# A softmax whose exponentials move from one instruction per step to one per row

## The chip, the cores and the metric

The kernel runs on one core of one Trainium2 chip. The metric is the device time of one execution in microseconds (us).

## What is computed

A gated cross-attention layer and a gated expert layer over x (32 sequences x 64 positions x 512), all in fp32 precision:

```python
x = x + tanh(g_xattn) * attention(layernorm(x), ctx, ctx, mask)
x = x + tanh(g_ffn) * lora_top1(layernorm(x))
# attention: 32 query heads and 8 key/value heads of width 128, rotary embedding on q and k
raw    = einsum('bhqd,bhkd->bhqk', q, k) / sqrt(128)
attn   = softmax(raw + mask, axis=-1)        # over 64 keys
out    = einsum('bhqk,bhkd->bhqd', attn, v) @ wo
```

The softmax of one row of 64 scores is: find the maximum, subtract it, take exponentials, add them up, divide by the sum.

## The kernel before

The program is written with one instruction list per engine and semaphores between them. Engines are TensorE (PE, with its weight loads PEld), VectorE (DVE), ScalarE (ACT), GpSimd (POOL) and the DMA queue of SyncE (SP). Each list is executed in the order in which it is written. So an instruction that waits holds up all that stands behind it in its list.

Matmuls in fp32 precision are made of three products of a "high" half, which ACT writes as a rounded copy, and a "low" half, which DVE or POOL writes as the rest (`*_high`, `*_low`).

**First part (to about 238 us).** `JOBS`, 64 of them: keys and values of all sequences are made and stored in DRAM, and x is normalised, combined and turned. Beside them stand splits of the weights.

**Second part: 64 steps k** (`STEPS`). A step is one group of 4 heads, 4 sequences of 64 positions. Its scores fill one tile `prob` of 128 x 512: 128 partitions (two heads x 64 queries) and `ROWS` = 8 rows of 64 keys each. There is one such tile, and its steps reuse it. The steps are pipelined by one. In step k the lists hold, in this order:

- PE: `scores(k)` (L784), `times_values(k-1)` (L811, L815), one or two blocks of `product` (L767: the queries of the next group of heads), `project_out(k-1, 0)` (L829), in even steps another `product`, `turn_probs(k)` (L795: transposes `prob`, and waits for `normalised`), `project_out(k-1, 1)`, the last `product`.
- DVE: `mask_scores(k)` (L1030 scale and mask, L1033 the negated maximum of each row), `attn_low(k-1)` twice (L1053, which `project_out` waits for), `sum_rows(k)` (L1037 the sums, L1039 their reciprocals), `q_sum` (L1011), `add_out` (L1065, waits for `project_out`), `q_rope` (L969, L974), `prob_low` twice (L1046), `add_out`, `q_rope`.
- ACT: `attn_high(k-1)` twice (L1290), in even steps `copy_product` (L1266), `exponential(k)` (L1274), `wq_split` (L1237) in even steps, `q_shift` (L1244, L1245), in even steps `copy_product`, `prob_high(k)` (L1281, L1282: four instructions), `q_shift`, and further copies and splits.
- POOL: `subtract_max(k)` (L1437), in the even steps to 24 `combine_weights` (L1396 to L1401), `normalise(k)` (L1442), in the first 26 steps `weight_low` (L1406), `by_sin` (L1431, which `q_rope` waits for).

The softmax of step k thus goes over three engines: DVE finds the maxima, POOL adds the negated maxima to the tile, ACT takes all 512 exponentials of a partition in one instruction, DVE adds up the rows and inverts the sums, POOL multiplies. From step 26 on no weights are left to be split. Steps 30 to 33 and 62 and 63 also hold parts of the expert layer, and steps 60 to 63 have no `product`.

Of the kernel before, what the change touches and what calls it, by code (L numbers as in the profile page):

```python
# [10 lines left out]
ACT = mybir.ActivationFunctionType  # L11
AX = mybir.AxisListType

P = 128
BATCH, SEQ, DM = 32, 64, 512
# [24 lines left out]
ROWS = HEAD_PAIRS * SUB_SEQS  # L40
# [115 lines left out]
def sums_of(k):  # L156

    early, middle, late = products_of(k)
    done = [i for b, i in early]
    after = [i for b, i in late]  # L160
    b = (early or [(0, 0)])[0][0]
    return ([(b, j) for j, s in enumerate(SUMS) if s[1] in done], [(b, j) for j, s in enumerate(SUMS) if s[1] in after])


def ropes_of(k):

    early, late = sums_of(k)
    pending = sums_of(k - 1)[1] if k else [(1, 3)]
    pending = [q for q in pending if q[1] == 3]
    rest = [q for q in late if q[1] != 3]  # L170
    if len(early) == 2:
        return early[:1], early[1:], rest
    return pending, early, rest
# [6 lines left out]
SCORES_AFTER = 62  # L180
# [67 lines left out]
def wo_late(k):  # L248

    G, r = divmod(k, 4)  # L250
    lot = [[GROUP * G + 2, GROUP * G + 3] if G else [], [GROUP * G + 4], [GROUP * G + 5], []][r]
    return [n for n in lot if n < HEADS] if G < KV_HEADS else []


def build(nc, x, ctx_T, mask, g_attn, g_ffn, wq, wk, wv, wo, routed_w, lora_b, table, out):
# [10 lines left out]
    with ExitStack() as stack:  # L266
# [3 lines left out]
        def sem(name):  # L270
            return stack.enter_context(nc.semaphore(name))

        def sb_at(offset, name, shape, dt=F32):
            return nc.alloc_sbuf_tensor_at(name, shape, dt, offset=offset)
# [30 lines left out]
        prob = sb_at(base + 141312, "prob", [P, 512])  # L305
# [3 lines left out]
        def sb(name, shape, dt=F32):  # L309
            offset = cursor[0]  # L310
            cursor[0] += (4 * int(np.prod(shape[1:])) + 31) // 32 * 32
            return sb_at(offset, name, shape, dt)
# [15 lines left out]
        neg_max = sb("neg_max", [P, 2, ROWS])  # L328
        row_sum = sb("row_sum", [P, 2, ROWS])
# [34 lines left out]
        shifted, exponentials, probs_high, v_high = sem("shifted"), sem("exponentials"), sem("probs_high"), sem("v_high")  # L364
# [3 lines left out]
        raw_low_v, x_low, q_summed = sem("raw_low_v"), sem("x_low"), sem("q_summed")  # L368
        ln_stats, ln_moments, ln_var, ln_done = sem("ln_stats"), sem("ln_moments"), sem("ln_var"), sem("ln_done")
        times_cos, rope_added, masked, max_found = sem("times_cos"), sem("rope_added"), sem("masked"), sem("max_found")  # L370
        summed, inverted, probs_low, v_low = sem("summed"), sem("inverted"), sem("probs_low"), sem("v_low")
        out_low, x1_added = sem("out_low"), sem("x1_added")
        top_found, top_ranked, rank_found, weight_set = sem("top_found"), sem("top_ranked"), sem("rank_found"), sem("weight_set")
        weighted, out_ready = sem("weighted"), sem("out_ready")

        power_set, ln_rstd, times_sin, less_max = sem("power_set"), sem("ln_rstd"), sem("times_sin"), sem("less_max")
        normalised, raw_low_g, wq_low = sem("normalised"), sem("raw_low_g"), sem("wq_low")
        wq_combined, x_combined = sem("wq_combined"), sem("x_combined")

# [548 lines left out]
        def _(e):  # L928
# [90 lines left out]
            by_row = prob[:, :].rearrange("p (r k) -> p r k", r=ROWS)  # L1019

            def mask_scores(k):
                u, s = divmod(k, SUBS)
                G, c, index = chunk_of(u)
                m = mask_sb[:, c, s * SUB_SEQS:(s + 1) * SUB_SEQS, :].rearrange("p b k -> p (b k)").unsqueeze(1).to_broadcast(
                    [P, HEAD_PAIRS, SUB_SEQS * SEQ])
                e.wait_ge(scored, k + 1)
                e.wait_ge(mask_in[c], 16 * (index // CHUNKS + 1))
                if k:
                    e.wait_ge(probs_turned, k)
                e.scalar_tensor_tensor(out=by_head, in0=score[:, :].rearrange("p (h n) -> p h n", h=HEAD_PAIRS),  # L1030
                                       scalar=SCALE, in1=m, op0=ALU.mult, op1=ALU.add).then_inc(masked, 1)
                e.wait_ge(masked, k + 1)
                e.tensor_reduce(neg_max[:, k % 2, :], by_row, AX.X, ALU.max, negate=True).then_inc(max_found, 1)  # L1033

            def sum_rows(k):
                e.wait_ge(exponentials, k + 1)
                e.tensor_reduce(row_sum[:, k % 2, :], by_row, AX.X, ALU.add).then_inc(summed, 1)  # L1037
                e.wait_ge(summed, k + 1)
                e.reciprocal(row_inv[:, k % 2, :], row_sum[:, k % 2, :]).then_inc(inverted, 1)  # L1039

            def prob_low(k):
# [71 lines left out]
            for n in range(len(JOBS)):  # L1113
# [17 lines left out]
                    x_lows(X_BESIDE[n - X_TURN])  # L1131
                if n == SCORES_AFTER:
                    mask_scores(0)
            sum_rows(0)
            for k in range(STEPS):
                early, late = sums_of(k)
                ropes = ropes_of(k)
                if k:
                    mask_scores(k)
                    attn_low(k - 1, 0)  # L1140
                    attn_low(k - 1, 1)
                    for n in wo_late(k - 1):
                        raw_low(("wo", n))
                    expert_norms_end(norms_of(k - 1))
                between(k, 0)
                between(k, 1)
                if k:
                    sum_rows(k)
                for q in early:
                    q_sum(*q)  # L1150
                between(k, 2)
                if k:
                    add_out(k - 1, 0)
                between(k, 3)
                for q in ropes[0]:
                    q_rope(*q)
                between(k, 4)
                prob_low(k)
                between(k, 5)
                if k:  # L1160
                    add_out(k - 1, 1)
                between(k, 6)
                for q in ropes[1]:
                    q_rope(*q)
                for q in late:
                    if q[1] != 3:
                        q_sum(*q)
                between(k, 7)
                for q in ropes[2]:
                    q_rope(*q)  # L1170
                for q in late:
                    if q[1] == 3:
                        q_sum(*q)
                between(k, 8)
                expert_norms_begin(norms_of(k))
            k = STEPS
# [18 lines left out]
        def _(e):  # L1195
# [74 lines left out]
                shift(ROPE_NO["q", b, j], q_tile(b, j))  # L1270

            def exponential(k):
                e.wait_ge(less_max, k + 1)
                e.activation(prob[:, :], prob[:, :], ACT.Exp).then_inc(exponentials, 1)  # L1274

            def prob_high(k):
                e.wait_ge(probs_turned, k + 1)
# [45 lines left out]
            for k in range(STEPS):  # L1323
                first, middle, last = products_of(k)
# [45 lines left out]
        def _(e):  # L1370
# [61 lines left out]

            by_row = prob[:, :].rearrange("p (r k) -> p r k", r=ROWS)

            def subtract_max(k):
                e.wait_ge(max_found, k + 1)
                e.tensor_tensor(by_row, by_row, neg_max[:, k % 2, :].unsqueeze(2).to_broadcast([P, ROWS, SEQ]),  # L1437
                                ALU.add).then_inc(less_max, 1)

            def normalise(k):  # L1440
                e.wait_ge(inverted, k + 1)
                e.tensor_tensor(by_row, by_row, row_inv[:, k % 2, :].unsqueeze(2).to_broadcast([P, ROWS, SEQ]),  # L1442
# [5 lines left out]
            for n in range(len(JOBS)):  # L1448
                for w in SPLITS_BESIDE.get(n, ()):
                    raw_low(w)  # L1450
                if n in X_BESIDE:
                    x_norms(X_BESIDE[n])
                if n in COMBINED_BESIDE:
                    combine_weights(COMBINED_BESIDE[n])
                for w in WQ_BESIDE.get(n, ()):
                    weight_low(*w)
                if JOBS[n][0] == "k":
                    by_sin(ROPE_NO[JOBS[n]])
                if n in ROPE_BESIDE:
                    by_sin(ROPE_NO["q", *ROPE_BESIDE[n]])  # L1460
                if n in X_BESIDE:
                    combine_x(X_BESIDE[n])
                if n == SCORES_AFTER:
                    subtract_max(0)
            normalise(0)
            for k in range(STEPS):
                ropes = ropes_of(k)
                pieces = weights_of(k)
                if k:
                    subtract_max(k)  # L1470
                if pieces and k % 2 == 0:
                    combine_weights(pieces[0][0])
                if pieces and k % 4 == 3:
                    weight_low(*pieces[0])
                if k:
                    normalise(k)
                if pieces and k % 4 != 3:
                    weight_low(*pieces[0])
                for q in ropes[0]:
                    by_sin(ROPE_NO["q", *q])  # L1480
                if pieces:
                    weight_low(*pieces[1])
                for q in ropes[1] + ropes[2]:
                    by_sin(ROPE_NO["q", *q])
                for n in wo_late(k):
                    raw_low(("wo", n))
                for t in norms_of(k):
                    inverse_std(("expert", t))
# [45 lines left out]
```

## Time and profile before

| | |
|---|---|
| median of 3 runs | 1208.34 us (1205.32 to 1209.72) |
| profiled execution | 1204.42 us, span 1202.4 us |
| mean granted TensorE clock | 0.981 |
| busy | PE 94%, PEld 77%, DVE 76%, ACT 53%, POOL 47% of the span |

The span is what the profile covers. The busy share of an engine is its busy time over the span. "Idle before" is the time that an engine stood still ahead of an instruction, and the arrow names what ended it. In the timeline each row is one instruction, or several of a kind in a row (x2, x4): start in us from the span's start, duration, engine and line, and what is written and read with the shape.

### The profile page before, as it was taken

What the parts mean: (1) busy time and instruction counts of PE and PEld (TensorE: products, weight loads), DVE (VectorE), ACT (ScalarE), POOL (GpSimd) and SP (SyncE); (2) the same over time, 40 slices, a digit from 0 to 9 for tenths busy, and PEclk for the clock granted to TensorE, in tenths of its full rate; (3) what the DMA queues carried; (4) which work ended last, traced back from release to release, by engine and by line L of the source; (5) the groups of instructions that cost most, each with busy time, mean ns of one, the idle gap of its engine ahead of it and who ended that gap; (6) DMA issues with size and microseconds to landing.
All of it is one profiled execution on the core that took longest, in us unless ns stands there. A gap on an engine that the chain in (4) does not pass through costs nothing.

```text
span 1202.4 us, 17218 instructions
## 1 busy us (share of the span) xinstructions
PE 1134.0 (94%) x5792; PEld 929.5 (77%) x5792; DVE 916.3 (76%) x1408; ACT 632.8 (53%) x1090; POOL 567.8 (47%) x517
## 2 busy tenths in 40 slices
PE   7899899879999999999999999999999999999786
PEld 6688787767777777777878777888888888887664
DVE  6773756768777777777888898887878888888574
ACT  6452345555666666666665544555555555545331
POOL 4650468766767676766654332333333333333210
PEclk9899999889999999999999999999999999999897
DMA  6859954384444454535359435453433424241101
GB/s 220 249 196 369 316 182 179 123 323 144 176 168 175 153 182 135 184 132 185 114 219 355 161 123 160 145 195 107 158 106 140 165 90 158 88 158 34 47 27 44
DMA packets 88902, 197.89 MB, mean 165 GB/s; under 512 B 8304, under 2 KB 41200, under 8 KB 82928
## 3 DMA queue, kind: packets, MB, share of 16 engines
q1 hardware_dynamic: 88816, 196.79, 47.7%
q8 instruction: 48, 0.79, 0.3%
q14 instruction: 38, 0.31, 0.1%
HBM read 113.92 MB, written 82.84 MB: 164 GB/s over the span
## 4 chain that ended last, share of the span: by engine, by line
PE 52%; DVE 15%; POOL 14%; issue 11%; ACT 4%; DMA 1%; SPq 1%; DVEq 0%; POOLq 0%; ACTq 0%
PE attn L829 19%; PE proj L767 13%; POOL rot L1431 4%; PE score L784 4%; PE attn L719 4%; DVE o_s L1053 2%; PE score L719 2%; DVE q_r L969 2%; POOL wq_s L1406 2%; PE turned L719 2%; DVE p_low L1046 2%; DVE acc L1065 2%; PE turned L795 2%; DVE prob L1030 1%; ACT p_high L1282 1%
## 5 line engine op out<-in xcount | busy, mean ns | idle before, releaser
L829 PE MATMUL attn<-wo_s,o_s 128*128 128x512 f32 x1536 | 388.8, 402 | 17.1 <-DVE o_s L1053 17.1
L829 PEld LDWEIGHTS attn<-wo_s,o_s 128*128 128x128 f32 x1536 | 283.3, 190 | 89.3 <-DVE o_s L1053 32.7
L767 PE MATMUL proj<-xB,wq_s 128*128 128x512 f32 x1344 | 344.9, 400 | 6.8 <-DVE q_r L1011 3.5
L1431 POOL TENSOR_TENSOR rot<-rot,tab 128x512 f32<-128x512 f32 x160 | 215.0, 1345 | 224.2 <-ACT rot L1245 224.1
L767 PEld LDWEIGHTS proj<-xB,wq_s 128*128 128x128 f32 x1344 | 249.3, 189 | 67.9 <-DVE q_r L1011 4.4
L974 DVE TENSOR_TENSOR q_r<-q_r,rot 128x512 f32<-128x512 f32 x128 | 125.1, 978 | 52.6 <-POOL rot L1431 41.6
L1437 POOL TENSOR_TENSOR prob<-prob,neg_max 128x512 f32<-128x512 f32 x64 | 66.9, 1045 | 179.9 <-DVE neg_max L1033 179.9
L1290 ACT ACTIVATE o_s<-attn 128x512 fp32r<-128x512 f32 x128 | 69.6, 596 | 149.1 <-PE attn L815 149.0
L1065 DVE SCALAR_TENSOR_TENSOR acc<-attn,gates_t,acc 128x512 f32<-128x512 f32 x128 | 96.1, 751 | 67.3 <-PE attn L829 65.3
L969 DVE TENSOR_TENSOR q_r<-q_r,tab 128x512 f32<-128x512 f32 x128 | 136.0, 1063 | 3.1 <-ACT rot L1245 3.0
L784 PEld LDWEIGHTS score<-k_r,q_r 128*128 128x128 f32 x1024 | 124.1, 191 | 7.0 <-issue 2.4
L784 PE MATMUL score<-k_r,q_r 128*128 128x64 f32 x1024 | 121.1, 271 | 0.0
L1244 ACT ACTIVATE rot<-q_r 64x512 f32<-64x512 f32 x128 | 80.8, 631 | 62.5 <-DVE q_r L1011 55.5
L1046 DVE TENSOR_TENSOR p_low<-turned,p_high 64x512 fp32r<-64x512 f32 x128 | 87.8, 686 | 30.7 <-ACT p_high L1282 29.1
L1442 POOL TENSOR_TENSOR prob<-prob,row_inv 128x512 f32<-128x512 f32 x64 | 66.9, 1046 | 85.5 <-DVE row_inv L1039 85.5
L1266 ACT ACTIVATE copies<-proj 128x512 f32<-128x512 f32 x96 | 57.5, 599 | 91.2 <-PE proj L767 91.0
L1281 ACT ACTIVATE p_high<-turned 64x512 fp32r<-64x512 f32 x128 | 76.0, 593 | 33.5 <-PE turned L795 29.6
L1011 DVE TENSOR_TENSOR q_r<-copies,proj 128x512 f32<-128x512 f32 x128 | 84.2, 678 | 0.8 <-PE proj L767 0.6
L1274 ACT ACTIVATE prob<-prob 128x512 f32<-128x512 f32 x64 | 40.4, 632 | 83.4 <-POOL prob L1437 83.4
L1053 DVE TENSOR_TENSOR o_s<-attn,o_s 128x512 fp32r<-128x512 f32 x128 | 81.9, 681 | 0.2 <-ACT o_s L1290 0.2
L1245 ACT ACTIVATE rot<-q_r 64x512 f32<-64x512 f32 x128 | 80.7, 631 | 1.5
L1282 ACT ACTIVATE p_high<-turned 64x512 fp32r<-64x512 f32 x128 | 76.0, 594 | 1.5
(118 smaller groups left out, 1398.9 us busy)
## 6 DMA issues: line engine op xcount, KB each, us to landing
wq_kept<-wq_s SPq DMA_DIRECT2D x16, 1792.0 KB, 6.5
wq_s<-wq_kept SPq DMA_DIRECT2D x16, 1792.0 KB, 8.3
v_kept<-vst SPq DMA_DIRECT2D x64, 256.0 KB, 4.1
v_s<-v_kept SPq DMA_DIRECT2D x128, 128.0 KB, 4.9
wo_kept<-wo_s SPq DMA_DIRECT2D x32, 512.0 KB, 2.9
wo_s<-wo_kept SPq DMA_DIRECT2D x32, 512.0 KB, 5.3
k_kept<-kst SPq DMA_DIRECT2D x32, 256.0 KB, 2.1
wq_raw<-in_wq SPq DMA_DIRECT2D x16, 512.0 KB, 7.8
```

The costliest lines, as they stand in the source:

```text
L719: last = e.matmul(b[:, :], stationary, moving, start=(kt == 0 and m == 0), stop=(kt == KT - 1 and m == 2))
L767: last = e.matmul(dst[:, :], wq_s[:, b % 2, A, s, kt, :], xB[:, B, mv, kt, :], start=(first and kt == 0 and m == 0), stop=(kt == 1 and m = ...
L784: last = e.matmul(score[:, col:col + SEQ], two_heads, k_r[:, u % 2, seq * SEQ:(seq + 1) * SEQ], start=True, stop=True)
L829: last = e.matmul(attn[bp][:, :], o_s[:, s, bp, h, :], wo_s[n % WO_SLOTS][:, m, :], start=(h == 0 and i == 0), stop=(h == GROUP - 1 and i ...
L969: e.tensor_tensor(dst, src, cos, ALU.mult).then_inc(times_cos, 1)
L974: e.tensor_tensor(dst, dst, by_seq(rotated(r)), ALU.add).then_inc(rope_added, 1)
L1011: e.tensor_tensor(q_tile(b, j), by_seq(copies[:, copy, :]), by_seq(proj[PRODUCTS[i][2]][:, :]), ALU.add).then_inc(q_summed, 1)
L1046: e.tensor_tensor(p_low[rows, :], turned[rows, :], p_high[rows, twin, :].bitcast(F32), ALU.subtract).then_inc(probs_low, 1)
L1053: e.tensor_tensor(low, src, high.bitcast(F32), ALU.subtract).then_inc(out_low, 1)
L1065: e.scalar_tensor_tensor(out=acc[:, tile, :], in0=attn[bp][:, :], scalar=gates_t[:, 0:1], in1=acc[:, tile, :], op0=ALU.mult, op1=ALU.add). ...
L1282: e.activation(p_high[rows, twin, :], turned[rows, :], ACT.Copy).then_inc(probs_high, 1)
L1431: e.tensor_tensor(r3, r3, sin, ALU.mult).then_inc(times_sin, 1)
```

## The change

The three passes over the tile (subtraction on POOL, one exponential on ACT, sums on DVE) are replaced by eight ACT instructions, one for each row of 64. Each takes the row's negated maximum as a per-partition bias and writes the row's sum as a second result. The reciprocals (L1039) and the multiplication (L1442) stay. The semaphores `less_max` and `summed` go.

```diff
             def exponential(k):
-                e.wait_ge(less_max, k + 1)
-                e.activation(prob[:, :], prob[:, :], ACT.Exp).then_inc(exponentials, 1)
+                e.wait_ge(max_found, k + 1)
+                for r in range(ROWS):
+                    here = prob[:, r * SEQ:(r + 1) * SEQ]
+                    last = e.activation(here, here, ACT.Exp, bias=neg_max[:, k % 2, r:r + 1],
+                                        accum_out=row_sum[:, k % 2, r:r + 1])
+                last.then_inc(exponentials, 1)
...
-            def sum_rows(k):
+            def invert_sums(k):
                 e.wait_ge(exponentials, k + 1)
-                e.tensor_reduce(row_sum[:, k % 2, :], by_row, AX.X, ALU.add).then_inc(summed, 1)
-                e.wait_ge(summed, k + 1)
                 e.reciprocal(row_inv[:, k % 2, :], row_sum[:, k % 2, :]).then_inc(inverted, 1)
...
-            def subtract_max(k):
-                e.wait_ge(max_found, k + 1)
-                e.tensor_tensor(by_row, by_row, neg_max[:, k % 2, :].unsqueeze(2).to_broadcast([P, ROWS, SEQ]),
-                                ALU.add).then_inc(less_max, 1)
...
-                if n == SCORES_AFTER:
-                    subtract_max(0)
...
-                if k:
-                    subtract_max(k)
```

The call `sum_rows(k)` becomes `invert_sums(k)` at the same place of DVE's list, and `exponential(k)` keeps its place in ACT's.

## Rows read from the trace of the kernel before

**Rows 1.** The page's busy times: us, share of span, instructions.

```profile
PE 1134.0 (94%) x5792; PEld 929.5 (77%) x5792; DVE 916.3 (76%) x1408; ACT 632.8 (53%) x1090; POOL 567.8 (47%) x517
```

**Rows 2.** Waits: who waited for whom, us in total, times, longest.

```profile
ACT prob L1274 <- POOL prob L1437: 83.4, 63, 2.6
...
DVE row_sum L1037 <- ACT prob L1274: 31.1, 50, 0.8
...
PE attn L829 <- DVE o_s L1053: 17.1, 30, 2.8
```

**Rows 3.** Groups of instructions: count, busy us, mean ns, idle before.

```profile
L1437 POOL TENSOR_TENSOR prob<-prob,neg_max 128x512 f32<-128x512 f32 x64 | 66.9, 1045 | 179.9 <-DVE neg_max L1033 179.9
L1037 DVE TENSOR_REDUCE row_sum<-prob 128x8 f32<-128x512 f32 x64 | 43.9, 686 | 31.3 <-ACT prob L1274 31.1
L1274 ACT ACTIVATE prob<-prob 128x512 f32<-128x512 f32 x64 | 40.4, 632 | 83.4 <-POOL prob L1437 83.4
```

**Rows 4.** Timeline of step 23 (odd, first half), the softmax's chain, by engine.

```profile
576.08 0.69 DVE L1033 TENSOR_REDUCE neg_max<-prob 128x8 f32<-128x512 f32 x1
576.69 1.28 DVE L1053 TENSOR_TENSOR o_s<-attn,o_s 128x512 fp32r<-128x512 f32 x2
578.59 0.69 DVE L1037 TENSOR_REDUCE row_sum<-prob 128x8 f32<-128x512 f32 x1 [0.62 <-ACT prob L1274]
579.31 0.20 DVE L1039 RECIPROCAL row_inv<-row_sum 128x8 f32<-128x8 f32 x1
581.12 0.75 DVE L1065 SCALAR_TENSOR_TENSOR acc<-attn,gates_t,acc 128x512 f32<-128x512 f32 x1 [0.41 <-PE attn L829]
...
576.85 1.04 POOL L1437 TENSOR_TENSOR prob<-prob,neg_max 128x512 f32<-128x512 f32 x1 [1.95 <-DVE neg_max L1033]
579.59 1.04 POOL L1442 TENSOR_TENSOR prob<-prob,row_inv 128x512 f32<-128x512 f32 x1 [0.46 <-DVE row_inv L1039]
...
577.93 0.63 ACT L1274 ACTIVATE prob<-prob 128x512 f32<-128x512 f32 x1 [2.15 <-POOL prob L1437]
580.14 0.63 ACT L1244 ACTIVATE rot<-q_r 64x512 f32<-64x512 f32 x1 [1.58 <-DVE q_r L1011]
581.55 0.59 ACT L1281 ACTIVATE p_high<-turned 64x512 fp32r<-64x512 f32 x1
```

**Rows 5.** Timeline of PE, from step 22 into step 24.

```profile
567.23 0.60 PE L795 MATMUL turned<-tab,prob 128*128 128x128 f32 x4
...
580.92 0.60 PE L795 MATMUL turned<-tab,prob 128*128 128x128 f32 x4
...
591.71 3.01 PE L829 MATMUL attn<-wo_s,o_s 128*128 128x512 f32 x12 [0.33 <-DVE o_s L1053]
```

**Rows 6.** Maximum and turn, steps 3 (first half), 22 (even), 59 (second half).

```profile
285.88 0.69 DVE L1033 TENSOR_REDUCE neg_max<-prob 128x8 f32<-128x512 f32 x1
290.72 0.60 PE L795 MATMUL turned<-tab,prob 128*128 128x128 f32 x4
...
561.07 0.69 DVE L1033 TENSOR_REDUCE neg_max<-prob 128x8 f32<-128x512 f32 x1
...
1097.40 0.69 DVE L1033 TENSOR_REDUCE neg_max<-prob 128x8 f32<-128x512 f32 x1
1102.48 0.60 PE L795 MATMUL turned<-tab,prob 128*128 128x128 f32 x4
```

**Rows 7.** ACT's small forms, and two instructions of one form in a row.

```profile
L1314 ACT ACTIVATE gates_t<-gates 128x2 f32<-128x2 f32 x1 | 0.2, 203 | 0.0
L1237 ACT ACTIVATE wq_s<-wq_raw 128x256 fp32r<-128x256 f32 x16 | 6.4, 401 | 0.0
...
574.69 1.09 ACT L1290 ACTIVATE o_s<-attn 128x512 fp32r<-128x512 f32 x2 [0.55 <-PE attn L815]
```

**Rows 8.** Timeline of DVE in step 31, which holds parts of the expert layer.

```profile
697.23 0.69 DVE L1033 TENSOR_REDUCE neg_max<-prob 128x8 f32<-128x512 f32 x1
701.30 0.20 DVE L1039 RECIPROCAL row_inv<-row_sum 128x8 f32<-128x8 f32 x1
```

More of the change, by code:

```diff
@@ L370, in build @@
         times_cos, rope_added, masked, max_found = sem("times_cos"), sem("rope_added"), sem("masked"), sem("max_found")
-        summed, inverted, probs_low, v_low = sem("summed"), sem("inverted"), sem("probs_low"), sem("v_low")
+        inverted, probs_low, v_low = sem("inverted"), sem("probs_low"), sem("v_low")
         out_low, x1_added = sem("out_low"), sem("x1_added")
@@ L374, in build @@
         weighted, out_ready = sem("weighted"), sem("out_ready")
-        power_set, ln_rstd, times_sin, less_max = sem("power_set"), sem("ln_rstd"), sem("times_sin"), sem("less_max")
+        power_set, ln_rstd, times_sin = sem("power_set"), sem("ln_rstd"), sem("times_sin")
         normalised, raw_low_g, wq_low = sem("normalised"), sem("raw_low_g"), sem("wq_low")
@@ L1133, in _ @@
                     mask_scores(0)
-            sum_rows(0)
+            invert_sums(0)
             for k in range(STEPS):
@@ L1147, in _ @@
                 if k:
-                    sum_rows(k)
+                    invert_sums(k)
                 for q in early:
```

## The prediction

> **What bounds the kernel now.** I read the busy times first. PE is busy for 1134.0 us, 94% of the span, ACT for 53%, POOL for 47% [rows 1]. So work taken from POOL (one pass) or DVE (one pass) is worth nothing by itself. Only what makes PE wait, or ends a wait of PE, moves the end. The table of waits says how little PE waits: its matmuls lose 17.1 us to `o_s` of DVE [rows 2], and in its timeline the turn of the probabilities has no idle time ahead of it [rows 5]. The waits inside the softmax (ACT for POOL 83.4 us, DVE for ACT 31.1 us) look large [rows 2], but they lie on engines with room.
>
> So the question is one of slack: how early is `prob` normalised, before PE reaches the turn? The timeline answers it for each step. In step 23 the maxima are ready at 576.08 + 0.69 = 576.77, the tile is normalised at 579.59 + 1.04 = 580.63 [rows 4], and PE turns it at 580.92 [rows 5]. The chain takes 3.86 us of the 4.15 that PE gives it. The reader is to see that PE comes to the turn from `project_out` without a gap, and that only 0.3 us stand between. Three kinds of step, each repeating within 0.05 us:
> - odd steps of the first half (3 to 29, 14 steps): room 4.15 us (step 3: 286.57 to 290.72) [rows 6];
> - odd steps of the second half (35 to 61, 14 steps): 4.39 us (step 59: 1098.09 to 1102.48) [rows 6];
> - even steps (27 of the usual kind): 5.47 us (step 22: 561.76 to 567.23), since one more product stands before the turn [rows 5, 6].
>
> **What the change removes from the chain.** In the order of rows 4: POOL's pass 1.04, the hand-over 0.04, the exponential 0.63, the hand-over 0.03, DVE's sums 0.69. Together 2.43 us. What stays: 0.08 to start, 0.03, the reciprocal 0.20, 0.08, the multiplication 1.04, together 1.43. Let B be the time from the first to the end of the last of the eight instructions with their sums. The new chain is B + 1.43, and **B = 2.43 us is break-even for the chain**. The turn needs one more hand-over, 0.06 (those of rows 4 take 0.03 to 0.08).
>
> **What B is.** No row of before has a 64-wide instruction on ACT, a pointer as bias, or a sum as second result, so B is bounded. Alone, an instruction of 2 columns takes 203 ns and one of 256 takes 401 [rows 7]; a line through both gives 0.25 us at 64. Narrowing a tile eightfold thus saves only 0.38 of the 0.63 us [rows 3], and eight are to be issued. Two of a form in a row take 1.09 us where each takes 0.596, so a joint saves 0.10. The spacing s of two rows is then at least 0.25 - 0.10 = 0.15 (bias and sum free), B = 8 x 0.15 + 0.10 = 1.3 us. At the other end the sum must be handed out after the last element: priced as one more small instruction, 0.20, and the bias as another 0.20, with no joint saved, s = 0.65 and B = 5.3 us. Between, with the sum a small instruction and one joint saved, s = 0.35. I add about a third of a small instruction for the bias and take **s = 0.42, B = 8 x 0.42 + 0.10 = 3.46 us**. That is nearest to the small-instruction row: a second result is at least a write of its own, and 0.20 is the smallest write that the rows show.
>
> The Trainium skill has a price for a part of this: on the page "ScalarE: Activation LUTs", section "What ACT_TABLE_LOAD costs", an instruction with immediates takes 186 ns + 0.833 ns a column (399 at 256 columns; the row's 401 agrees), a pointer operand adds 93 ns, and neighbours overlap by 93. By it s would be 0.24 and B 2.0 us if the sum cost nothing, and by that the chain would be shorter than before; it gives no price for the sum. The page "VectorE: DVE Perf Modes", section "The TRN2 errata", speaks against the change: ScalarE pays its fixed latency once for each instruction, and tiles should have 512 elements or more; the same page says in "Two Vector instructions with no wait between them" that an accumulator output makes two instructions of one on VectorE, and no row here shows whether ScalarE does so.
>
> **What it costs, at B = 3.46.** The turn comes at B + 1.43 + 0.06 = 4.95 us behind the maxima.
> - First-half odd: 4.95 - 4.15 = 0.80 us of waiting PE. Part comes back: the next `project_out` waited 0.33 us for DVE anyway [rows 5]. But DVE is late too. Its wait for the exponentials holds up all behind it: the reciprocal, both query sums, `add_out`, the ropes, and through them the next mask and `o_s`. The reciprocal starts at B + 0.11 = 3.57 instead of 2.54 us, 1.03 later, and 0.41 of it is absorbed where DVE waited for PE before L1065 [rows 4], leaving 0.62. I take 0.70 a step.
> - Second-half odd: 4.95 - 4.39 = 0.56; about 0.50 with the same give.
> - Even: 4.95 < 5.47, nothing. In the first half POOL's four combinations used to stand between subtraction and multiplication; the freed POOL does them earlier, and DVE's later start is covered by its waits for PE and for POOL.
> - Steps 31 to 34: DVE has other work there and inverts at 701.30 - 697.92 = 3.38 us behind the maxima [rows 8]. New 3.57, so 0.2 each, 0.8 together.
>
> ACT itself has room: it gets 64 x (3.46 - 0.63) = 181 us more, (632.8 + 181)/1202 = 68%. DVE loses 43.9 us and POOL 66.9 [rows 3], hidden under PE and worth 0. If the cover were gone (a chain no longer than now), DVE's 0.69 a step could only buy back PE's 17.1 us of waits.
>
> Sum: 14 x 0.70 + 14 x 0.50 + 0.8 = 17.6 us. The profiled execution took 1204.4 us, so 1222; it lies 3.9 us under the median of the runs, so the predicted median is 1208.3 + 17.6 = **1226 us**.
>
> **The rivals.**
> 1. *As forecast, B 3.1 to 4.1.* Only odd steps stretch: 1216 to 1241 us.
> 2. *The delay counts in full.* In an odd step ACT goes from the exponentials to `q_shift`, which waits for a query sum behind DVE's reciprocal, and from there straight to `p_high` (580.14, then 581.55 [rows 4]). Once the query sum is there no idle time is left between them, so everything may shift by B - 2.43 = 1.03 us in 28 steps: +29, 1237 us. Against it: the next mask finds DVE's wait for PE to hide in.
> 3. *The sum is dear, B above 4.1.* At s = 0.57, B = 4.66: odd steps wait 2.00 and 1.76 us (with the give 1.9 and 1.7, 50 us together), and even ones 4.66 + 1.49 - 5.47 = 0.68 (27 x 0.68 = 18). +69 with the 1 us of the expert steps, 1278 us. At the bound B = 5.3 it is 14 x (2.6 + 2.4) + 27 x 1.3 = 105, so 1313 us.
> 4. *The sum is nearly free, B 2.0 to 3.0.* The chain fits in its room (4.15 - 1.49 = 2.66), no step stretches by more than 0.3: 1208 us, at most 1213. For it: ACT has idle time, and nothing in the rows says that a second result costs an instruction. The price in the Trainium skill ("ScalarE: Activation LUTs") of the pointer with a free sum lands here.
> 5. *Faster.* With B below 2.0 the reciprocal comes 0.4 us earlier or more, and DVE is a whole pass shorter. Then mask, maxima and `o_s` of the next step come earlier, and PE's 17.1 us of waits for them [rows 2] go, half or all: 1192 to 1200 us. It decides only below break-even, B < 2.43; against it, nothing in the rows shows that DVE's spare time reaches the `o_s` that PE waits for, with ropes and PE's own results between.
>
> **How the numbers follow.** Chances: 1: 0.34; 2: 0.12; 3: 0.20; 4: 0.23; 5: 0.11. A measurement of this kernel tells 0.5% (6 us) from no change. Rivals 1 to 3 are slower by more than that, 0.66; 4 is the same, 0.23; 5 is faster, 0.11. The range goes down to 1203, which takes in rival 4 and the edge of 5, and up to 1278, s = 0.57; outside are about 0.08 below and 0.08 above.
>
> **What would show it.** In the timeline of an odd step: eight rows instead of one on ACT, possibly with an instruction for the sum beside each; B from the first's start to the reciprocal. The turn L795 in odd steps should carry an idle time that ends with POOL's multiplication, some 0.5 to 0.8 us, and none in even ones. DVE's reciprocal should show the wait for ACT, about 2.4 us a step (3.57 - 1.19 for `o_s`) instead of 0.6. ACT should be busy about 68%. Two steps together should take about 0.7 us longer than before in the first half, 0.5 in the second. The prediction is wrong if s is under 0.36 or over 0.50, or if the delay of DVE's list spreads further than the turn's.

## The result, and the profile after

The changed kernel takes 1213.8 us (median of 6 runs, 1212.93 to 1217.73) against 1208.15 us before (6 runs): ratio **1.0059**, 95% interval 1.0039 to 1.0080. It is slower, by 5.7 us of medians and 7 us by the ratio, where 17.6 was forecast. The profiled execution took 1212.9 us (span 1211.1), 8.5 us over the one before. Runs of one kernel differ by some us with the mean granted TensorE clock (three runs of the changed kernel at 0.982 took 1213.0 us, one at 0.975 took 1217.7), and as the two profiled executions had 0.982 and 0.981, their 8.5 us are the closer measure of what the change costs.

The page's busy times of the changed kernel stand first, against [rows 1]:

```profile
PE 1137.0 (94%) x5792; PEld 929.1 (77%) x5792; DVE 900.9 (74%) x1344; ACT 766.4 (63%) x2050; POOL 513.5 (42%) x453
```

ACT is busy for 134 us more, not 181. POOL loses 54 us, though 66.9 us of passes are gone, and DVE only 15 of 43.9 [rows 3]: both engines have become slower at something else. The groups of instructions name it (mean ns behind the busy us; in the last column the idle time before them):

```profile
L1275 ACT ACTIVATE prob<-prob,neg_max 128x64 f32<-128x64 f32 x512 | 170.8, 336 | 27.0 <-DVE neg_max L1033 26.4
L1275 ACT ACTIVATION_READ_ACCUMULATOR prob<-prob,neg_max 128x1 f32 x512 | 96.3, 188 | 0.0
L969 DVE TENSOR_TENSOR q_r<-q_r,tab 128x512 f32<-128x512 f32 x128 | 159.2, 1244 | 4.5 <-ACT rot L1243 4.3
L974 DVE TENSOR_TENSOR q_r<-q_r,rot 128x512 f32<-128x512 f32 x128 | 129.9, 1015 | 44.5 <-POOL rot L1434 34.7
```

The same two groups of DVE before:

```profile
L969 DVE TENSOR_TENSOR q_r<-q_r,tab 128x512 f32<-128x512 f32 x128 | 136.0, 1063 | 3.1 <-ACT rot L1245 3.0
L974 DVE TENSOR_TENSOR q_r<-q_r,rot 128x512 f32<-128x512 f32 x128 | 125.1, 978 | 52.6 <-POOL rot L1431 41.6
```

The rope's two passes, which the change doesn't touch, cost DVE 28 us more. And each exponential comes with an instruction of its own that reads the sum. The block of step 23, in ACT's timeline:

```profile
583.26 0.35 ACT L1275 ACTIVATE prob<-prob,neg_max 128x64 f32<-128x64 f32 x1 [0.93 <-DVE neg_max L1033]
583.52 0.19 ACT L1275 ACTIVATION_READ_ACCUMULATOR prob<-prob,neg_max 128x1 f32 x1
583.61 0.33 ACT L1275 ACTIVATE prob<-prob,neg_max 128x64 f32<-128x64 f32 x1
...
585.85 0.19 ACT L1275 ACTIVATION_READ_ACCUMULATOR prob<-prob,neg_max 128x1 f32 x1
586.90 0.63 ACT L1242 ACTIVATE rot<-q_r 64x512 f32<-64x512 f32 x1 [0.86 <-DVE q_r L1011]
```

From one row to the next it is 0.33 us: the reading starts 0.24 behind its exponential (0.26 for the first) and the next exponential 0.09 behind the reading. B is 586.04 - 583.26 = 2.78 us, where 3.46 was taken. DVE and POOL in the same step (compare [rows 4]), and PE (compare [rows 5]):

```profile
582.54 0.69 DVE L1033 TENSOR_REDUCE neg_max<-prob 128x8 f32<-128x512 f32 x1
586.07 0.20 DVE L1037 RECIPROCAL row_inv<-row_sum 128x8 f32<-128x8 f32 x1 [1.64 <-ACT prob L1275]
...
587.54 0.75 DVE L1063 SCALAR_TENSOR_TENSOR acc<-attn,gates_t,acc 128x512 f32<-128x512 f32 x1
...
590.07 1.77 DVE L974 TENSOR_TENSOR q_r<-q_r,rot 128x512 f32<-128x512 f32 x1 [1.18 <-POOL rot L1434]
...
593.86 1.25 DVE L969 TENSOR_TENSOR q_r<-q_r,tab 128x512 f32<-128x512 f32 x1
595.22 1.04 DVE L974 TENSOR_TENSOR q_r<-q_r,rot 128x512 f32<-128x512 f32 x1
...
586.35 1.04 POOL L1440 TENSOR_TENSOR prob<-prob,row_inv 128x512 f32<-128x512 f32 x1 [3.28 <-DVE row_inv L1037]
588.25 1.79 POOL L1434 TENSOR_TENSOR rot<-rot,tab 128x512 f32<-128x512 f32 x1 [0.85 <-ACT rot L1243]
...
593.84 0.73 POOL L1400 TENSOR_TENSOR combined<-wq_raw 128x256 f32<-128x256 f32 x1
594.53 1.18 POOL L1402 TENSOR_TENSOR combined<-combined,wq_raw 128x256 f32<-128x256 f32 x1
...
587.45 0.66 PE L795 MATMUL turned<-tab,prob 128*128 128x128 f32 x4
...
599.43 3.02 PE L829 MATMUL attn<-wo_s,o_s 128*128 128x512 f32 x12 [1.24 <-DVE o_s L1051]
```

The maxima are ready at 583.23, the reciprocal starts 2.84 us later (before 2.54), the tile is normalised 4.16 us later (before 3.86), and PE turns 4.22 us later (before 4.15). PE does not wait at the turn: its row has no idle time ahead of it. It waits at the next `project_out`, 1.24 us instead of 0.33 [rows 5], for an `o_s` that DVE makes late. That is 0.91 of the 1.27 us by which this step grew. Ahead of this `o_s` DVE's ropes take 1.25 and 1.04 us, and beside them POOL runs its combinations. In the kernel before, the same two passes took 0.68 and 0.69 us (starts 587.06 and 587.85). There the combinations stood behind the subtraction, so they could not begin before the maxima of the next step (590.46), when the ropes were done:

```profile
591.54 0.73 POOL L1396 TENSOR_TENSOR combined<-wq_raw 128x256 f32<-128x256 f32 x1
```

Measured from mask to mask (starts of L1030), in us:

| | before | after |
|---|---|---|
| steps 2, 4 ... 26 | 14.97 to 15.04 | 14.91 to 14.97 |
| steps 3, 7 ... 23 | 13.68 | 14.95 to 14.96 |
| steps 5, 9 ... 21 | 14.30 to 14.32 | 14.86 to 14.88 |
| odd steps 37 to 59 | 13.35 to 13.36 (one of 13.70) | 13.34 to 13.37 |
| steps 2 to 30 together | 406.4 | 416.2 |
| steps 30 to 63 together | 477.1 | 477.2 |

The second half has no combinations and no splits of weights, and there the change costs nothing.

### The profile page after: what moved, and what is told of

It is laid out like the page before. It is cut to its first block, busy times and chain, and to the rows that moved or that the text cites. A ratio compares the mean times of both kernels' runs of the same rounds, so it can differ in the third digit from the quotient of the medians.

```text
span 1211.1 us, 18050 instructions
## 1 busy us (share of the span) xinstructions
PE 1137.0 (94%) x5792; PEld 929.1 (77%) x5792; DVE 900.9 (74%) x1344; ACT 766.4 (63%) x2050; POOL 513.5 (42%) x453
## 4 chain that ended last, share of the span: by engine, by line
PE 49%; DVE 20%; POOL 11%; issue 10%; ACT 8%; DMA 1%; SPq 1%; DVEq 0%; ACTq 0%; POOLq 0%
PE attn L829 17%; PE proj L767 13%; ACT prob L1275 5%; POOL rot L1434 5%; PE score L784 4%; DVE q_r L969 4%; PE attn L719 4%; DVE p_low L1044 3%; POOL wq_s L1409 2%; DVE acc L1063 2%; PE score L719 2%; PE turned L719 2%; DVE prob L1030 2%; DVE neg_max L1033 2%; POOL prob L1440 2%
## 5 line engine op out<-in xcount | busy, mean ns | idle before, releaser
L1434 POOL TENSOR_TENSOR rot<-rot,tab 128x512 f32<-128x512 f32 x160 | 224.5, 1404 | 219.3 <-ACT rot L1243 219.0
L1275 ACT ACTIVATE prob<-prob,neg_max 128x64 f32<-128x64 f32 x512 | 170.8, 336 | 27.0 <-DVE neg_max L1033 26.4
L974 DVE TENSOR_TENSOR q_r<-q_r,rot 128x512 f32<-128x512 f32 x128 | 129.9, 1015 | 44.5 <-POOL rot L1434 34.7
L969 DVE TENSOR_TENSOR q_r<-q_r,tab 128x512 f32<-128x512 f32 x128 | 159.2, 1244 | 4.5 <-ACT rot L1243 4.3
L1063 DVE SCALAR_TENSOR_TENSOR acc<-attn,gates_t,acc 128x512 f32<-128x512 f32 x128 | 96.1, 751 | 46.9 <-PE attn L829 43.6
L1275 ACT ACTIVATION_READ_ACCUMULATOR prob<-prob,neg_max 128x1 f32 x512 | 96.3, 188 | 0.0
L1284 ACT ACTIVATE p_high<-turned 64x512 fp32r<-64x512 f32 x128 | 75.9, 593 | 28.0 <-PE turned L795 24.5
L1037 DVE RECIPROCAL row_inv<-row_sum 128x8 f32<-128x8 f32 x64 | 13.0, 203 | 100.1 <-ACT prob L1275 99.8
L1011 DVE TENSOR_TENSOR q_r<-copies,proj 128x512 f32<-128x512 f32 x128 | 84.1, 677 | 1.4 <-PE proj L767 0.6
L1051 DVE TENSOR_TENSOR o_s<-attn,o_s 128x512 fp32r<-128x512 f32 x128 | 81.8, 680 | 0.2 <-ACT o_s L1293 0.2
```

What stands on the lines that cost most here:

```text
L969: e.tensor_tensor(dst, src, cos, ALU.mult).then_inc(times_cos, 1)
L974: e.tensor_tensor(dst, dst, by_seq(rotated(r)), ALU.add).then_inc(rope_added, 1)
L1011: e.tensor_tensor(q_tile(b, j), by_seq(copies[:, copy, :]), by_seq(proj[PRODUCTS[i][2]][:, :]), ALU.add).then_inc(q_summed, 1)
L1063: e.scalar_tensor_tensor(out=acc[:, tile, :], in0=attn[bp][:, :], scalar=gates_t[:, 0:1], in1=acc[:, tile, :], op0=ALU.mult, op1=ALU.add). ...
L1275: last = e.activation(here, here, ACT.Exp, bias=neg_max[:, k % 2, r:r + 1], accum_out=row_sum[:, k % 2, r:r + 1])
L1434: e.tensor_tensor(r3, r3, sin, ALU.mult).then_inc(times_sin, 1)
```

## The experiments

All ratios are to the kernel before on the same chip, with 95% intervals. The sum of steps 2 to 30 comes from the profiled execution, and it leaves out the head of the program, which varies by several us. In all profiled executions the granted clock was full in these steps. Two explanations are set against each other. Theory C: the freed POOL runs its combinations earlier, beside DVE's ropes, and both get slower. Rival L: the later reciprocal and turn stretch the odd steps.

**The gate (e1).** POOL waits for the maxima where its subtraction stood, and does nothing for them:

```diff
                 pieces = weights_of(k)
+                if k:
+                    e.wait_ge(max_found, k + 1)
                 if pieces and k % 2 == 0:
                     combine_weights(pieces[0][0])
```

> POOL waits for the maxima of step k again, at the place where its subtraction stood, and does nothing for them; all else is the changed kernel. Theory C (the freed POOL runs its combinations and splits earlier, beside DVE's ropes, and both get slower): POOL's L1396-type combinations start behind the maxima again, DVE's L969 falls from 1244 ns to about 1060, the steps of the first half that grew (14.95 and 14.87 us) fall back to within 0.3 us of 13.68 and 14.3, and the time goes to 1202 to 1208 us. Rival L (the lateness of reciprocal and turn on the chain, 0.3 us a step, is what stretches the odd steps): the chain is as long as in the changed kernel, so the time stays at 1212 to 1216 us.

Measured: **1.0018** (1.0003 to 1.0032); steps 2 to 30 in 409.5 us, steps 3, 7 ... at 14.02, steps 5, 9 ... at 14.60. DVE at the end of step 23:

```profile
587.64 0.68 DVE L969 TENSOR_TENSOR q_r<-q_r,tab 128x512 f32<-128x512 f32 x1
588.42 0.69 DVE L974 TENSOR_TENSOR q_r<-q_r,rot 128x512 f32<-128x512 f32 x1
```

A wait without work takes 6.7 of the 9.8 us by which steps 2 to 30 had grown. In step 23 the two passes fall from 1.25 and 1.04 to 0.68 and 0.69 us, 0.92 together, and the step gets 0.93 us shorter. Over the whole kernel L969 fell only to 1222 ns, not to 1060 as expected: most of its lengthening lies where it costs the end nothing. Rival L had foreseen no gain from the gate, so it cannot explain the greater part. But 0.3 us stays in each odd step to step 25, and that is L's share.

**The early POOL without the new exponentials (e2).** The kernel before, with the same POOL work ahead of the subtraction:

```diff
-                if k:
-                    subtract_max(k)
                 if pieces and k % 2 == 0:
                     combine_weights(pieces[0][0])
                 if pieces and k % 4 == 3:
                     weight_low(*pieces[0])
+                if k:
+                    subtract_max(k)
```

> The kernel before, softmax in three passes, with POOL's combinations (even steps) and its first split (every fourth step) moved ahead of the subtraction, as the removal of the subtraction lets them run. Theory C: DVE's L969 and L974 get longer in the first half, odd steps grow by 0.5 to 1.3 us, and the time goes to 1214 to 1220 us without any change of the exponentials. Rival L: nothing on the chain is later (POOL is idle for 3 us ahead of the subtraction), so the time stays at 1207 to 1210 us.

Measured: **1.0027** (1.0008 to 1.0047), 409.7 us for steps 2 to 30. The order alone makes an untouched softmax slower, by 3.3 us, but not by the 6 to 12 that I had expected. In steps 2 to 30 the order costs 3.3 us by itself, the longer chain 3.1 (e1), the two together 9.8: 3.4 us belong to both at once. Step 23 shows where. In e2 DVE's L969 starts 0.16 us ahead of a combination and takes 0.76 us, and the combination takes 1.19. In the changed kernel DVE stands 0.2 us later against POOL's list: L969 starts 0.02 us behind a combination (593.86 and 593.84), and now it is L969 that gets long, 1.25 us, while the combination takes 0.73. L974 takes 1.04 us in both.

**Sums back on DVE (e3).** The eight instructions keep the bias and lose the second result; L1037's row sums return:

```diff
-                    last = e.activation(here, here, ACT.Exp, bias=neg_max[:, k % 2, r:r + 1],
-                                        accum_out=row_sum[:, k % 2, r:r + 1])
+                    last = e.activation(here, here, ACT.Exp, bias=neg_max[:, k % 2, r:r + 1])
...
+                e.tensor_reduce(row_sum[:, k % 2, :], by_row, AX.X, ALU.add).then_inc(summed, 1)
+                e.wait_ge(summed, k + 1)
```

> Eight exponentials with the bias, but no second result; DVE adds up the rows as in the kernel before. From the changed kernel's rows (the instruction 0.336 us, the next thing started 0.24 us behind it) the eight take 8 x 0.24 + 0.09 = 2.0 us instead of 2.76, and the chain gets DVE's 0.69 + 0.03 back: again about 4.15 us from maximum to normalised tile. Both theories expect the time of the changed kernel, 1212 to 1217 us; theory C a little more if DVE's extra 0.69 us a step counts in the steps that DVE now bounds (14 x 0.3 = 4 us). If it comes out at 1208, the accumulator reads cost something that neither has.

Measured: **1.0068** (1.0047 to 1.0088). An exponential still takes 336 ns, the eight together 2.02 us, the reciprocal starts 2.81 us behind the maxima, and steps 2 to 30 take 415.5 us. So at this tile size reading eight sums on ACT (0.75 us) and adding them on DVE (0.72 with its hand-over) cost the chain the same, and DVE's 44 us less work is worth nothing to the end. Both theories had this time, so this run does not decide between them.

**Gate and query sums (e4).** The kernel of e1, and DVE makes the query sums while it waits for ACT:

```diff
-                if k:
-                    invert_sums(k)
                 for q in early:
                     q_sum(*q)
+                if k:
+                    invert_sums(k)
```

> The gate of e1, and DVE does the query sums of the step ahead of the reciprocals, in the 1.6 us in which it waits for the exponentials. In odd steps two sums (1.27 us) fit, so what stands behind the reciprocal on DVE comes up to 1.2 us earlier, and ACT's shift is no longer late. Theory C: faster than e1 by 0 to 5 us (PE's waits for DVE's L1051 are what can still go), 1198 to 1206 us. Rival L: if DVE's lateness behind the reciprocal is the cause, this takes it away: 1203 to 1208 us against 1212 to 1216 of e1.

Measured: **0.9992** (0.9976 to 1.0008), 405.5 us. Steps 3, 7 ... fall from 14.02 to 13.25, though reciprocal and turn come no earlier than in e1. In these steps this shows the path of the last 0.3 us: ACT's shift waits for a query sum that stood behind the reciprocal, POOL's `by_sin` waits for the shift, and DVE's rope for `by_sin`. The changed kernel's rows of step 23 have it too. Counted from the maxima, `add_out` (L1063) starts 4.31 us behind them, where it started 4.35 behind them before: DVE itself is not late there. But the shift starts at 3.67 instead of 3.37, `by_sin` (L1434) at 5.02 instead of 4.72, and DVE then waits 1.18 us for it. Steps 5, 9 ... did not fall (14.67, in e1 14.60); their path is found in e8.

**The block almost as long as the prediction took it (e5).** The kernel of e1 with six small copies (8 columns, to a place of their own) ahead of the exponentials:

```diff
+PAD = 6
...
+                for r in range(PAD):
+                    e.activation(pad[:, r:r + 1, :], neg_max[:, k % 2:k % 2 + 1, :], ACT.Copy)
                 for r in range(ROWS):
```

> The kernel of e1 with six small ACT instructions (a copy of the 8 negated maxima to a place of their own) ahead of the eight exponentials of every step, to make the block as long as the prediction took it: 6 x about 0.11 us, so from maxima to reciprocal 3.5 us instead of 2.83. If the prediction's terms were right and only the length of the block was not, the turn waits now: odd steps of the first half reach 14.7 and 15.3 us (the delay in full, 1.0 us over the kernel before), odd steps of the second half 13.8 instead of 13.35, even steps stay; together 14 x 0.67 + 14 x 0.5 = 16 us over e1. If even steps grow too or the second half stays at 13.35, the terms were wrong as well.

Measured: **1.0148** (1.0120 to 1.0176). The reciprocal starts 3.42 us behind the maxima (forecast 3.57). Steps 3, 7 ... take 14.61, steps 5, 9 ... 15.18, odd steps of the second half 13.89, even ones 14.93 and 14.03. PE now waits at the turn, here in step 25, and 0.33 us in step 43:

```profile
617.70 0.66 PE L797 MATMUL turned<-tab,prob 128*128 128x128 f32 x4 [0.60 <-POOL prob L1444]
```

The ratio is 17.9 us on 1208, close to the 17.6 of the prediction, but at a shorter block: the lateness is 0.88 us and not 1.03. Over before, odd steps of the first half grew by 0.88 to 0.93 (0.70 was taken) and of the second half by 0.54 (0.50), and even ones not at all.

**Which POOL work it is (e6).** The gate in even steps alone holds back the combinations, not the split of steps 3, 7, 11:

```diff
-                if k:
+                if k and k % 2 == 0:
                     e.wait_ge(max_found, k + 1)
```

> The gate of e1 in even steps alone: it holds back the four combinations, but not the first split of every fourth step, L1409. Theory C says that it is the combinations beside L969 and L974 at the end of the odd steps: steps 2 to 30 take 409.5 to 410.5 us as in e1 (416.2 in the changed kernel). If the split counts (it ran at the start of the odd step, 1.74 us long beside the mask), they take 412 to 416.

Measured: **1.0020** (1.0004 to 1.0035), 409.0 us, where e1 took 409.5. It is the combinations. The 0.5 us are a cost of the gate itself: in steps 5, 9 ... POOL's multiplication ended 4.23 us behind the maxima in e1 and ends at 4.16 here, and these steps fall from 14.60 to 14.52.

**A better order on the new exponentials (e7, e8, e9).** Three kernels, the first two with the gate of e1. In the first (e7), only odd steps make query sums ahead:

```diff
+                ahead = k % 2 * (1 if k % 4 == 1 else 2)
+                for q in early[:ahead]:
+                    q_sum(*q)
                 if k:
                     invert_sums(k)
-                for q in early:
+                for q in early[ahead:]:
                     q_sum(*q)
```

> The kernel of e1 with query sums ahead of the reciprocals in odd steps alone, as many as fit into DVE's wait for ACT (two, or one where a low half of wo is made there), so that the reciprocal is never later than the exponentials. Against e4 the reciprocal of even steps comes at 2.83 again instead of 3.34, that of steps 1, 5, 9 at 2.83 instead of 2.90. Expected: odd steps 13.24 as in e4's step 23 and 14.3 in step 21, steps 2 to 30 in 402 to 405.5 us, and the time 0.2 to 0.5% under the kernel before. If it equals e4 (405.5), the even order costs nothing.

Measured: **0.9979** (0.9966 to 0.9991), 404.6 us; steps 3, 7 ... 13.23, steps 5, 9 ... still 14.58, though 14.3 was expected. In these POOL goes from the multiplication through a split to `by_sin`. So in the second (e8) the split goes ahead of the multiplication there too:

```diff
-                if pieces and k % 4 == 3:
+                if pieces and k % 2 == 1:
                     weight_low(*pieces[0])
                 if k:
                     normalise(k)
-                if pieces and k % 4 != 3:
+                if pieces and k % 2 == 0:
                     weight_low(*pieces[0])
```

> The kernel of e7, and in steps 1, 5, 9 ... 25 too POOL makes its first split of the weights (L1412, 1.28 us) ahead of the multiplication of the probabilities, in the 3 us and more in which it waits for the reciprocal, as it does in steps 3, 7, 11. In e7 these steps take 14.57 us (before 14.30), and DVE's rope waits 1.19 us in them for POOL, which comes to it by multiplication and split. If POOL's order carries the lateness of the reciprocal on to the ropes there, they fall to 13.3 to 14.2 us, steps 2 to 30 to 395 to 402 us, and the time to 0.995 of the kernel before or less. If they stay at 14.5, something else holds them.

Measured: **0.9948** (0.9932 to 0.9964), 1199.7 us median; 402.1 us, steps 5, 9 ... at 14.13. So in these steps it was POOL's order that carried the late reciprocal on to the ropes. This is the fastest kernel of the study. The third (e9) is the same without the gate:

> The kernel of e8 without POOL's wait for the maxima, so that combinations and splits run as early as they can. Theory C: the combinations slow DVE's L969 and L974 at the end of odd steps again, by about 0.4 to 0.9 us a step where DVE sets the pace: steps 2 to 30 take 3 to 8 us longer than in e8. If the query sums ahead have given DVE enough room, the two agree within 1 us, and contention costs only a kernel whose DVE is late already.

Measured: **0.9971** (0.9960 to 0.9983), 404.0 us, 1.9 more than e8 where 3 to 8 were expected; steps 3, 7 ... take 13.58 instead of 13.24, and L974 in step 23 takes 1.03 us instead of 0.69. So even with the query sums ahead a step loses 0.34 us there.

**Do the rows earn it? (e10, e11)** The same changes of order on the three passes, as far as idle times allow:

```diff
+                ahead = 1 if k % 4 == 3 else 0
+                for q in early[:ahead]:
+                    q_sum(*q)
                 if k:
                     sum_rows(k)
-                for q in early:
+                for q in early[ahead:]:
                     q_sum(*q)
...
-                if pieces and k % 4 == 3:
+                if pieces and k % 2 == 1:
                     weight_low(*pieces[0])
...
-                if pieces and k % 4 != 3:
+                if pieces and k % 2 == 0:
                     weight_low(*pieces[0])
```

> The kernel before, exponentials in three passes, with the two changes of order of e8 as far as its idle times allow: one query sum ahead of the row sums in steps 3, 7, 11 ... (DVE waits 0.62 us there for ACT, and a sum takes 0.60), and POOL's first split ahead of the multiplication in all odd steps. It tells whether the gain of e8 (0.9948) needs the exponentials by row. If the order alone earns it: steps 2 to 30 in about 402 us and 0.995. If the waits for ACT, which are longer with exponentials by row, are what made the room: steps 3, 7, 11 at 13.2 us, steps 5, 9, 13 at 14.0 to 14.3 because the query sums there find no idle time, 398 to 403 us, so this kernel is as fast as e8 or up to 3 us faster, since its reciprocal comes 0.3 us earlier. If it stays at 406 us, the gain belongs to the rows.

Measured: **1.0031** (1.0017 to 1.0045), a miss. Steps 3, 7 ... reached 13.07, but steps 5, 9 ... went from 14.3 to 15.18. DVE and POOL in step 21:

```profile
548.44 1.81 DVE L964 TENSOR_TENSOR wo_s<-raw,wo_s 128x512 fp32r<-128x512 f32 x1
...
548.41 1.29 POOL L1409 TENSOR_TENSOR wq_s<-combined,wq_s 128x512 fp32r<-128x512 f32 x1
```

Behind the subtraction POOL's split starts 0.03 us ahead of a DVE pass that takes 0.68 us in the kernel before. Here it took 1.81 and made the row sums late. In e8, with no subtraction, the split begins a microsecond earlier against the same pass, and that pass takes 0.80. The last kernel (e11) keeps the query sum and drops the split:

> The kernel before with one change of order alone: in steps 3, 7, 11 ... one query sum ahead of the row sums. The kernel e10 had this and POOL's split ahead in steps 1, 5, 9; there steps 3, 7, 11 took 13.07 us (before 13.68) and steps 5, 9 took 15.18 (before 14.3), with DVE's L964 at 1.81 us instead of 0.68 beside the split that POOL started 0.03 us ahead of it. If it is that neighbourhood that costs, steps 5, 9, 13 are at 14.3 again, steps 2 to 30 take 406.4 - 7 x 0.6 = 402.2 us, and the time is 0.995 to 0.997 of the kernel before: as fast as e8, so that the exponentials by row earn nothing themselves. If the steps behind give the 0.6 us back (L964 slow or PE waiting elsewhere), it stays at 0.998 to 1.000.

Measured: **0.9982** (0.9967 to 0.9996), 402.7 us for steps 2 to 30. These steps are as fast as e8's 402.1. So for them the new exponentials are not needed. Over the whole, e8's interval lies below this one's. Of the 5.0 us between the two profiled executions 0.5 lie in steps 2 to 30, 1.8 in steps 0 and 1 (30.8 against 32.6), and 2.6 in steps 60 and 61 (26.0 against 28.6). These steps are the first without a `product`, and over the 45 us around them the mean granted clock was 0.89 of the full 2.4 GHz in e8 and 0.77 in e11. Whether that difference of clock comes from the order or from the execution was not settled. At the same mean clock of 0.982 e8 took 1199.0 us (two runs) and e11 1200.2 (one run), so it is not shown that the rows earn anything of their own.

## Why the prediction was off

**What held.** The chain's parts were right: 4.16 us measured, 2.78 + 1.43 = 4.21 by the formula. Even steps and, with B below 2.90, second-half odd steps don't stretch. That DVE's work is worth nothing to the end held too (e3). That PE waits at the turn in odd steps held only for the longer block of e5. In the changed kernel PE doesn't wait there, and the cost came another way: through DVE's list, for the greater part to the `o_s` that PE waits for. Two of the prediction's own signs of being wrong were met: s is under 0.36, and the delay of DVE's list spreads further than the turn's.

**Step that failed first: the length of the block.** "I ... take s = 0.42, B = 3.46" was 24% too long: s is 0.33 and B 2.78. The mis-sized term is the sum. It was priced as a small instruction of 0.20 us on top of 0.22 for an exponential with its bias. The rows show 0.24 for the exponential, and 0.09 for the sum. The sum is an instruction of its own, as was taken (188 ns), but it overlaps the exponential ahead of it by 0.10 us and the one behind it by 0.10 again, where the prediction saved one joint. With B = 2.78 the forecast's own terms give 14 x (4.27 - 4.15) = 1.7 us and nothing in the second half.

By the Trainium skill ("ScalarE: Activation LUTs", What ACT_TABLE_LOAD costs) an instruction with a pointer operand takes an estimated 280 + 0.833 x 64 = 333 ns at 64 columns, and the next may start 93 ns before its end, so after 0.24 us. The rows agree: 336 ns, and in e3, where exponentials follow each other directly, eight in 2.02 us, so 0.24 from one to the next.

**Step that failed second: the freed POOL.** "In the first half POOL's four combinations used to stand between subtraction and multiplication; the freed POOL does them earlier" was right, and it was priced at nothing. The removed instruction was also POOL's only wait for the maxima. Without it the combinations run beside DVE's ropes: 6.7 us (e1), of which 3.3 come without any change of the exponentials (e2).

**Step that was undervalued: the give.** I took 0.70 us of a 1.03 lateness in first-half odd steps, and rival 2 took it in full. Full is right, in these steps: 0.88 to 0.93 at 3.42 us (e5, lateness 0.88), about 0.3 at 2.83 (e1). The 0.41 us that DVE has to spare ahead of `add_out` did absorb its own lateness, but the query sums carried it round by ACT's shift and POOL's `by_sin` (e4). Rival 2 began with the same shift, and went on to `p_high` instead. In the second half the term was too small as well: at the block of e5 (B = 3.42 - 0.11 = 3.31) it gives 3.31 + 1.49 - 4.39 = 0.41 us less the give, and 0.54 was measured. All the forecast's terms together give some 13 us there, and 17.9 were measured, of which the gate may be a small part (e6). So at the block that the prediction took, its sum would have been too low.

So in steps 2 to 30 about 3 us of the cost are the later reciprocal, 3 to 4 the early combinations, and 3 to 4 the two together. Errors of opposite sign, a block too dear against a side effect at nothing and a give that was not there, met in part in the sum. That the time still lies inside the stated range is in part luck. B is in rival 4's region, and the time 0.8 us above its "at most 1213", for a reason that rival did not have.

## What to carry to other kernels

An instruction that is removed takes its waits along. Look at what stood behind it in its engine's list, how early that may start now, and what it will run beside. Where an engine gets a new wait, put work that is ready ahead of it: here this took the kernel from 1.0018 (e1) to 0.9948 (e8). And try the same order on the old version before giving the new one the credit.

## What the runs showed of the hardware

- A sum as second result is an instruction of its own on ScalarE: 188 ns, of which 0.09 us lengthen the sequence. A 64-column exponential with a pointer as bias takes 336 ns, a copy of 8 columns without one 196 (e5).
- VectorE passes with two inputs in SBUF, beside a GpSimd pass, went from 0.68 us to between 0.76 and 1.81. Passes with one input in PSUM kept their means from before to after (L1011 678 and 677 ns; L1053, now L1051, 681 and 680). GpSimd loses as well (L1402: 0.74 to 1.18 us). The Trainium skill ("SBUF — State Buffer", Who interferes with whom) says that a VectorE instruction with two SBUF inputs contends with GpSimd's reads and that issue order decides who is held; the rows agree, the 0.03 us of e10 most plainly.
